# Twelve decoder layers on one core: experts' weights loaded during the routing, two loops of one batch at a time staged side by side, and two steps of a cross-attention moved

## The chip, the core and the metric

The program runs on one core of a Trainium2 chip. The core has a matrix engine (PE, TensorE), a vector engine (DVE, VectorE), an activation engine (ACT, ScalarE), a general engine (POOL, GpSimd) and a queue engine (SP, SyncE) that issues the transfers. Each works through its own instructions in order and waits on semaphores for the others. The metric is the device time of one execution in microseconds (us), lower is better. The time of the kernel before is 4591.87 us, the median of 3 runs (4589.37 to 4594.4).

## What is computed

The reference runs x (16 batches of 128 rows by 256) through twelve sublayers, each `x = x + f(layernorm(x))`. The change touches four of them:

```
# L1_xattn: queries, keys, values from x and ctx rounded to fp8 steps, two attentions (over x, over ctx)
out = [attention(q, k, v), attention(qx, kx, vx)] @ wproj          # 16 + 16 heads of 128
# L1_ffn: one matrix of weights -1, 0, 1, input rounded to 8 bits
y = round(rmsnorm(x) * 127 / peak) @ ternary(W)
# L3_xattn: retention; A sums the scores over the batches, so all batches come before any output
A = max(abs(sum_over_batches(scores * decay)), 1);  out = relu(x @ wg) * groupnorm(A @ V) @ wo
# L3_ffn: 32 experts, 4 for each row, 32 places in each; the places are filled in the order of the rows
xe[expert, place] = x[row];  ye = (silu(xe @ Wg) * (xe @ Wu)) @ Wd;  out = shared(x) + sum(share * ye)
```

## The kernel before

`build_program` calls one function for each sublayer. All of x stays in on-chip memory (`kit.x`, `x_sb` in the profile), and a sublayer updates it in place, batch by batch. A `Phase` holds the tiles and semaphores of a stage; when it is closed, POOL clears the semaphores and all engines meet at a barrier. Within a stage every engine has a loop over the batches of its own (`Fori`), and the order is as written. `staged_by(eng, turn, lead)` calls a body for batches -lead to 15, two in each turn of the loop, so that a body can work on batch b, b+1 and b+2 in one call. `step(...)` makes DVE wait until its instruction has landed.

`L1_ffn` (from L1595) goes through one batch at a time: DVE normalises (L172), scales (L1653), quantises to `q` (L1418 to L1423), PE turns q (L1382), ACT copies it (L1635), PE multiplies (L1625), and DVE adds the result to x (L1657). Then the next batch begins.

`L1_xattn` (from L2492) has a long body for one batch. In its first half PE makes 12 groups of four heads (`make`, L2594) and four groups of values (`make_v`, L2600), DVE scales them to `hat`, PE turns them (`flip`, L2616), and ACT copies them to `hatT` (L2740). In the second half, eight groups m of four heads go through scores (L2624), maxima (L2910), exponentials (L2751, into a tile that the profile names `square`), the turn of P (L2634), its copy (L2757), the product with v (`mix`, L2642), the reciprocals of the sums (L2917), the rounding of the output and the projection. The queries of batch b+1 are turned by PE (`turn_x`, L1382) and copied with a scale by DVE (L2880) inside this half.

`L3_xattn` (from L2298) has two phases. The first loops over the batches and adds up the scores in two banks that stay open; context comes by one DMA per batch into one tile, and SP loads the next when the products of the last are made. The second phase loops again and makes the output; it is already staged by two.

`L3_ffn` (from L2970) has three phases: `L3r` routes (ranks the experts, finds the places, and gathers rows into `fill` banks by one-hot products), `L3e` runs the experts in 8 groups of four, with two slots for a group's weights, and `L3c` brings the results back and adds the shared expert.

Of the kernel before, what the change touches and what calls it, by code (L numbers as in the profile page):

```python
# [1594 lines left out]
def L1_ffn(kit):  # L1595
# [3 lines left out]
    with ExitStack() as ctx:  # L1599
# [6 lines left out]
        peak, scale = ph.sb("peak", [128, 1]), ph.sb("scale", [128, 1])  # L1606
# [9 lines left out]
        @block.tensor  # L1616
        def _(pe):
            w.tensor(kit, pe, bank[0][:, 0:1])
            pe.wait_ge(weights_ready, 1)
            with pe.Fori(0, B) as b:  # L1620
                pe.wait_ge(q_ready.sem, q_ready.after(b))
                turn_bf16(kit, pe, bank[1][:, 0:128].bitcast(BF16), q, C).then_inc(q_turned.sem, 1)
                pe.wait_ge(qT_ready.sem, qT_ready.after(b))
                for k in range(C):
                    last = pe.matmul(bank[2][:, 0:D], qT[:, k, :], w.q[:, k, :], start=(k == 0), stop=(k == C - 1))  # L1625
                last.then_inc(y_made.sem, 1)
# [11 lines left out]
        def _(dve):  # L1638
# [11 lines left out]
            with dve.Fori(0, B) as b:  # L1650
                step.restart()
                step(norm_vector(kit, dve, b, kit.xn[:, :]))
                step(dve.scalar_tensor_tensor(kit.xn[:, :], kit.xn[:, :], rms[:, bass.ds(b, 1)], gamma[:, :], ALU.mult, ALU.mult))  # L1653
                quantize_vector(dve, step, kit.xn[:, :], q[:, :], peak[:, :], scale[:, :], ALU.add, EPS).then_inc(q_ready.sem, 1)
                step(dve.tensor_scalar(peak[:, :], peak[:, :], 1.0 / 127.0, w.unit[:, :], ALU.mult, ALU.mult))
                dve.wait_ge(y_made.sem, y_made.after(b))
                step(dve.scalar_tensor_tensor(kit.x[:, bass.ds(b, 1), :], bank[2][:, 0:D], peak[:, :],  # L1657
                                              kit.x[:, bass.ds(b, 1), :], ALU.mult, ALU.add))
# [639 lines left out]
def L3_xattn(kit):  # L2298
# [4 lines left out]
    with ExitStack() as ctx:  # L2303
# [6 lines left out]
        qT, kT, ctxT = ph.sb("qT", [128, H, 128]), ph.sb("kT", [128, H, 128]), ph.sb("ctxT", [128, C, 128])  # L2310
# [7 lines left out]
        @block.sync  # L2318
        def _(sp):
            sp.dma_start(wh[:, :, :], kit.dram["L3_xattn_Wh"].rearrange("h p n -> p h n")).then_inc(loaded, 16)  # L2320
            sp.dma_start(decay[:, :, :], kit.dram["c_retention"]).then_inc(loaded, 16)
            with sp.Fori(0, B) as b:
                load_batch_T(sp, ctxT, kit.dram, b).then_inc(batch_loaded.sem, 16)
                end_turn(sp, qk_made, b, turns)

        @block.tensor
        def _(pe):
# [4 lines left out]
            with pe.Fori(0, B) as b:  # L2332
                pe.wait_ge(normed.sem, normed.after(b))
                turn_tensor(kit, pe, bank[0], kit.xn).then_inc(turned.sem, 1)
                pe.wait_ge(xT_ready.sem, xT_ready.after(b))
                pe.wait_ge(batch_loaded.sem, batch_loaded.after(b))
                for h in range(H):
                    pe.matmul(bank[1][:, h * 128:(h + 1) * 128], wh[:, h, :], kit.xnT[:, h, :], start=True, stop=True)
                    last = pe.matmul(bank[2][:, h * 128:(h + 1) * 128], wh[:, h, :], ctxT[:, h, :], start=True, stop=True)
                last.then_inc(qk_made.sem, 1)  # L2340
                pe.wait_ge(q_ready.sem, q_ready.after(b))
                pe.wait_ge(k_ready.sem, k_ready.after(b))
                for h in range(H):
                    last = pe.matmul(sums[h], kT[:, h, :], qT[:, h, :], start=False, stop=False)  # L2344
                last.then_inc(used.sem, 1)
# [5 lines left out]
        def _(act):  # L2351
            pre_norm.scalar(act)
            with act.Fori(0, B) as b:
                act.wait_ge(turned.sem, turned.after(b))
                act.copy(kit.xnT[:, :, :], bank[0][:, 0:D]).then_inc(xT_ready.sem, 1)
                act.wait_ge(qk_made.sem, qk_made.after(b))
                act.copy(qT[:, :, :], bank[1][:, 0:D]).then_inc(q_ready.sem, 1)

        @block.vector
        def _(dve):  # L2360
# [3 lines left out]
            with dve.Fori(0, B) as b:  # L2364
                norm_vector(kit, dve, b, kit.xn[:, :]).then_inc(normed.sem, 1)
                dve.wait_ge(qk_made.sem, qk_made.after(b))
                dve.tensor_copy(kT[:, :, :], bank[2][:, 0:D]).then_inc(k_ready.sem, 1)
                dve.wait_ge(used.sem, used.after(b))
# [23 lines left out]
        def _(sp):  # L2392
# [4 lines left out]
            with sp.Fori(0, B) as b:  # L2397
                load_batch_T(sp, ctxT, kit.dram, b).then_inc(batch_loaded2.sem, 16)
                end_turn(sp, v_made, b, turns)

        @second.tensor
        def _(pe):
# [3 lines left out]
            def turn(b, odd, at_b):  # L2406
                ahead, entering = 0 <= at_b + 1 < B, at_b + 2 < B
                if entering:
# [3 lines left out]
                    for h in range(H):  # L2412
                        last = pe.matmul(bank[1][:, h * 128:(h + 1) * 128], ctxT[:, h, :], wh[:, h, :], start=True, stop=True)
# [78 lines left out]
def L1_xattn(kit):  # L2492
# [12 lines left out]
    with ExitStack() as ctx:  # L2505
# [40 lines left out]
        v_bank = (bank[7], bank[0], bank[7], bank[0])  # L2546
# [25 lines left out]
        def _(pe):  # L2572
# [37 lines left out]
            def batch(b, last_batch=False):  # L2610
# [52 lines left out]
                for n in range(4, NG):  # L2663
# [10 lines left out]
                    if n >= 10:  # L2674
                        pe.wait_ge(v_ready.sem, v_ready.after(b, n - 9))
                        make_v(n - 8)
# [4 lines left out]
                flip(NG - 1)  # L2681
# [773 lines left out]
```

## Time and profile before

| | us |
|---|---|
| median of 3 runs | 4591.87 |
| the profiled execution's own time | 4596.84 |
| its span, first to last instruction | 4594.7 |
| PE busy, DVE busy, ACT busy in the span | 3417.8, 2701.4, 1742.3 |
| `L1_xattn`: turned queries copied, first and last batch | 1418.5, 2568.4 |
| `L1_ffn`: first statistics to last update | 2683.2 to 2786.1 |
| `L3_xattn`: first phase, second phase | 3776.1 to 3885.1, 3885.6 to 3976.1 |
| `L3_ffn`: routing, experts, bringing back begins | 3977.8 to 4222.3, 4223.3 to 4348.7, 4349.5 |

The span is what the profiler saw of one execution; the execution's own time has the start and the end around it, 2.1 us here. Starts are counted from the span's beginning. "Busy" of PE is modelled for the end of a matmul, so rows of PE overlap by a little.

### The profile page before, as it was taken

To read this page: it belongs to the slowest core of one execution; us is meant where nothing else is said; L and a number is where in the kernel's file an instruction comes from. 1 tells how busy PE (TensorE), PEld (TensorE's weight loads), DVE (VectorE), ACT (ScalarE), POOL (GpSimd) and SP (SyncE) were. 2 spreads that over 40 slices of the span, in tenths; PEclk is the share of its full clock that TensorE was granted. 3 is DMA by queue.
4 is the path that set the end of the run, shared out by engine and by line. 5 is a ranking of instruction groups with operands and counts; after the bars stand their busy time and mean duration, and the time that the engine had idled before them with its cause. 6 is when DMAs were issued, how large, how long until landed. Compare 5 with 4: busy or idle time off the path is not lost. (4 is left out here: it accounts for less than half of the span.)

```text
span 4594.7 us, 79435 instructions
## 1 busy us (share of the span) xinstructions
PE 3417.8 (74%) x29440; PEld 2478.0 (54%) x29440; DVE 2701.4 (59%) x6762; ACT 1742.3 (38%) x3873; POOL 87.5 (2%) x85
## 2 busy tenths in 40 slices
PE   5588888343776989898988936867767976665798
PEld 4455555211554666665656524656666754433687
DVE  4445555688667767676777666666722761675032
ACT  2233333366224666666666622233322431200011
POOL 0000000000000000000000000000000000000000
PEclk9799999655887999999999967977888995866599
DMA  0000000000300000000000000000000000001400
GB/s 30 30 19 19 20 19 14 32 0 0 126 9 2 1 2 1 2 1 2 1 2 1 1 4 17 4 23 11 9 20 22 0 4 29 24 0 38 132 0 18
DMA packets 85790, 79.54 MB, mean 17 GB/s; under 512 B 12704, under 2 KB 78849, under 8 KB 85121
## 3 DMA queue, kind: packets, MB, share of 16 engines
q1 hardware_dynamic: 85632, 77.21, 5.5%
q8 instruction: 127, 2.08, 0.2%
q14 instruction: 31, 0.25, 0.0%
HBM read 75.09 MB, written 2.10 MB: 17 GB/s over the span
## 5 line engine op out<-in xcount | busy, mean ns | idle before, releaser
L2594 PE MATMUL bank<-L1w_w,L1x_xqT 128*128 128x512 f32 x640 | 305.4, 601 | 1.4 <-DVE L1x_xqT L2880 1.4
L2657 PE MATMUL bank<-L1w_wp,L1x_catT 128*128 128x256 f32 x1024 | 247.4, 385 | 13.2 <-ACT L1x_catT L2768 13.2
L180 PE MATMUL bank<-ident,xn 128*128 128x128 f32 x320 | 77.4, 328 | 219.8 <-DVE xn L172 210.2
L2886 DVE TENSOR_REDUCE L1x_ssq<-L1x_square 128x4 f32<-128x512 f32 x192 | 131.6, 685 | 145.9 <-ACT L1x_square L2730 142.0
L2657 PEld LDWEIGHTS bank<-L1w_wp,L1x_catT 128*128 128x128 f32 x1024 | 188.5, 193 | 43.9 <-ACT L1x_catT L2768 16.1
L760 ACT ACTIVATE L0x_P<-bank 128x512 f32<-128x512 f32 x256 | 132.2, 602 | 190.3 <-PE bank L710 190.3
L2762 ACT ACTIVATE L1x_cat<-bank,L1x_osum 128x128 f32<-128x128 f32 x512 | 146.4, 368 | 152.6 <-DVE L1x_osum L2917 152.6
L776 DVE TENSOR_REDUCE L0x_top<-bank 128x4 f32<-128x512 f32 x256 | 159.0, 684 | 73.4 <-PE bank L688 71.6
L180 PEld LDWEIGHTS bank<-ident,xn 128*128 128x128 f32 x320 | 36.7, 154 | 272.0 <-issue 119.9
L2730 ACT ACTIVATE L1x_square<-bank 128x512 f32<-128x512 f32 x192 | 115.3, 600 | 155.8 <-PE bank L2594 155.8
L2594 PEld LDWEIGHTS bank<-L1w_w,L1x_xqT 128*128 128x128 f32 x640 | 114.0, 192 | 97.1 <-issue 91.4
L2740 ACT ACTIVATE L1x_hatT<-bank,L1x_affine 128x512 f32<-128x512 f32 x192 | 148.6, 774 | 39.3 <-PE bank L2616 37.3
L2616 PEld LDWEIGHTS bank<-ident,L1x_hat 128*128 128x128 f32 x768 | 88.7, 141 | 135.1 <-DVE L1x_hat L2896 96.0
L613 DVE TENSOR_TENSOR x_sb<-x_sb,bank 128x256 f32 (+1 forms) x112 | 47.0, 419 | 193.2 <-PE bank L197 186.6
L172 DVE TENSOR_SCALAR xn<-x_sb,meanvar,rstd 128x256 f32 (+1 forms) x208 | 87.7, 422 | 110.6 <-PE bank L2344 28.3
L2751 ACT ACTIVATE L1x_square<-bank,L1x_top 128x128 f32<-128x128 f32 x512 | 148.5, 397 | 0.0
L2616 PE MATMUL bank<-ident,L1x_hat 128*128 128x128 f32 x768 | 119.4, 278 | 33.9 <-DVE L1x_hat L2896 33.4
L2642 PE MATMUL bank<-L1x_v,L1x_PT 128*128 128x129 f32 x1024 | 140.3, 281 | 0.0
L2924 DVE TENSOR_TENSOR L1x_cat<-L1x_cat,L1x_smooth 128x512 f32<-128x512 f32 x128 | 88.6, 692 | 86.0 <-ACT L1x_cat L2762 86.0
L2896 DVE TENSOR_TENSOR L1x_hat<-bank,L1x_inv 128x512 f32<-128x512 f32 x192 | 132.8, 692 | 9.3
L2624 PE MATMUL bank<-L1x_hatT 128*128 128x128 f32 x1024 | 136.9, 279 | 0.0
L3039 PE MATMUL bank<-L3r_send,L3r_xn 128*128 128x512 f32 x128 | 102.8, 978 | 42.2 <-DVEq L3115 42.2
(642 smaller groups left out, 8173.7 us busy)
## 6 DMA issues: line engine op xcount, KB each, us to landing
L0x_mask<-in_maskrows SPq DMA_DIRECT2D x16, 512.0 KB, 3.6
L3e_wg<-in_L_ffn_Wg SPq DMA_DIRECT2D x8, 704.0 KB, 4.6
L3e_wu<-in_L_ffn_Wu SPq DMA_DIRECT2D x8, 704.0 KB, 6.5
L1w_wp<-in_L_xattn_wproj SPq DMA_DIRECT2D x1, 4096.0 KB, 29.8
L3x_ctxT<-in_ctxT SPq DMA_DIRECT2D x32, 128.0 KB, 2.1
L3e_wd<-in_L_ffn_Wd SPq DMA_DIRECT2D x8, 512.0 KB, 7.8
x_sb<-in_x SPq DMA_DIRECT2D x16, 128.0 KB, 2.2
L0x_ctxT<-in_ctxT SPq DMA_DIRECT2D x16, 128.0 KB, 2.2
```

The costliest lines, as they stand in the source:

```text
L760: act.activation(self.P[:, i % 2, r, :], self.work_bank[r][:, :], ACT.Exp).then_inc(self.p_ready.sem, 1)
L776: dve.tensor_reduce(self.top[:, s, 16 * c + 4 * r:16 * c + 4 * r + 4], self.work_bank[r][:, :].rearrange("p (h k) -> p h k", h=4), X, ALU.max,
L2594: last = pe.matmul(made_bank[n % 4][:, :], inputs(SOURCE[n], k), w[:, k, 4 * n:4 * n + 4, :], start=(k == 0), stop=(k == C - 1))
L2616: last = pe.transpose(flip_bank[n % 2][:, j * 128:(j + 1) * 128], hat[:, n % 2, j * 128:(j + 1) * 128], kit.ident[:, :])
L2624: last = pe.matmul(made_bank[m % 2][:, j * 128:(j + 1) * 128], hatT[:, q, :], hatT[:, k, :], start=True, stop=True)
L2642: last = pe.matmul(mix_bank[j // 2][:, (j % 2) * (d + 1):(j % 2 + 1) * (d + 1)], PT[:, m % 2, j * 128:(j + 1) * 128], v[:, g, :], start=Tr ...
L2657: last = pe.matmul(y_bank[:, 0:D], catT[:, j, :], wp[:, 4 * m + j, :], start=(m == 0 and j == 0), stop=(m == MG - 1 and j == 3))
L2740: act.activation(hatT[:, 4 * n:4 * n + 4, :], flip_bank[n % 2][:, :], ACT.Identity, scale=affine[:, 0, KIND[n]:KIND[n] + 1], bias=affine[: ...
L2751: last = act.activation(P[:, m % 2, j * 128:(j + 1) * 128], made_bank[m % 2][:, j * 128:(j + 1) * 128], ACT.Exp, bias=top[:, 4 * m + j:4 * ...
L2762: last = act.activation(cat[:, j * d:(j + 1) * d], mix_bank[j // 2][:, (j % 2) * (d + 1):(j % 2) * (d + 1) + d], ACT.Copy, scale=osum[:, j ...
L2886: dve.tensor_reduce(ssq[:, 4 * n:4 * n + 4], square[:, n % 2, :].rearrange("p (h e) -> p h e", h=4), X, ALU.add).then_inc(sum_ready.sem, 1)
L2896: dve.tensor_tensor(hat[:, n % 2, :].rearrange("p (h e) -> p h e", h=4), made_bank[n % 4][:, :].rearrange("p (h e) -> p h e", h=4), part.u ...
```

## The change

Five edits in four sublayers. (1) `L1_ffn` is staged by one: DVE prepares batch b+1 before it adds batch b; `peak` and the output bank are doubled. (2) In `L1_xattn` the last value product and the turn of the next batch's queries come after the last flip and ahead of the first turn of P; ACT keeps the last value group after the exponentials of m = 1; DVE copies the turned queries after the first two maxima; banks of the value groups 2 and 3 change places. (3) The first phase of `L3_xattn` is staged by two, with `qT`, `kT` and `ctxT` doubled; a load waits for the load before it and for the products of two batches back. The second phase uses the doubled `ctxT`. (4) In `L3_ffn` the weights have seven slots, in a phase `L3w` of their own around `L3r` and `L3e`; seven groups are loaded by SP during the routing, behind POOL's clearing of `wd1`, the eighth in `L3e`. (5) `L3e` is written out for the 8 groups, with two banks each for hidden and output; PE makes hidden(g+1) before it projects group g, and reads `xeT` directly.

```diff
@@ L1_ffn, tensor @@
-            with pe.Fori(0, B) as b:
+            with pe.Fori(0, B // 2) as t:
+                for i in range(2):
+                    b = t * 2 + i
...
-                    last = pe.matmul(bank[2][:, 0:D], qT[:, k, :], w.q[:, k, :], ...)
+                        last = pe.matmul(bank[2 + i][:, 0:D], qT[:, k, :], w.q[:, k, :], ...)
@@ L1_ffn, vector @@
+            def turn(b, odd, at_b):
+                here, ahead = at_b >= 0, at_b + 1 < B
                 step.restart()
+                if ahead:
+                    step(norm_vector(kit, dve, b + 1, kit.xn[:, :]))
+                    step(dve.scalar_tensor_tensor(kit.xn[:, :], kit.xn[:, :], rms[:, bass.ds(b + 1, 1)], gamma[:, :], ...))
+                    if here:
+                        dve.wait_ge(q_turned.sem, q_turned.after(b))
+                    part = peak[:, 1 - odd:2 - odd]
+                    quantize_vector(...).then_inc(q_ready.sem, 1)
+                    step(dve.tensor_scalar(part, part, 1.0 / 127.0, w.unit[:, :], ALU.mult, ALU.mult))
+                if here:
+                    dve.wait_ge(y_made.sem, y_made.after(b))
+                    step(dve.scalar_tensor_tensor(kit.x[:, bass.ds(b, 1), :], bank[2 + odd][:, 0:D], ...))
+            staged_by(dve, turn, 1)
@@ L3_xattn, sync (the second phase alike, with v_made) @@
-            with sp.Fori(0, B) as b:
-                load_batch_T(sp, ctxT, kit.dram, b).then_inc(batch_loaded.sem, 16)
-                end_turn(sp, qk_made, b, turns)
+            load(0, 0, batch_loaded)
+            sp.wait_ge(batch_loaded.sem, batch_loaded.after(0))
+            load(1, 1, batch_loaded)
+            with sp.Fori(0, (B - 2) // 2) as t:
+                for i in range(2):
+                    b = t * 2 + i
+                    sp.wait_ge(batch_loaded.sem, batch_loaded.after(b + 1))
+                    sp.sem_inc(turns, 1)
+                    sp.wait_ge(qk_made.sem, qk_made.after(b))
+                    sp.sem_inc(turns, 1)
+                    load(b + 2, i, batch_loaded)
@@ L3_xattn, scalar and vector @@
+                if ahead:
+                    act.wait_ge(qk_made.sem, qk_made.after(b + 1))
+                    act.copy(qT[:, 1 - odd, :, :], bank[1][:, 0:D]).then_inc(q_ready.sem, 1)
+                if entering:
+                    act.wait_ge(turned.sem, turned.after(b + 2))
+                    act.copy(kit.xnT[:, :, :], bank[0][:, 0:D]).then_inc(xT_ready.sem, 1)
...
+                    norm_vector(kit, dve, b + 2, kit.xn[:, :]).then_inc(normed.sem, 1)
+                if ahead:
+                    dve.wait_ge(qk_made.sem, qk_made.after(b + 1))
+                    dve.tensor_copy(kT[:, 1 - odd, :, :], bank[2][:, 0:D]).then_inc(k_ready.sem, 1)
@@ L1_xattn @@
-        v_bank = (bank[7], bank[0], bank[7], bank[0])
+        v_bank = (bank[7], bank[0], bank[0], bank[7])
...
                 flip(NG - 1)
+                pe.wait_ge(v_ready.sem, v_ready.after(b, 1))
+                make_v(3)
+                if not last_batch:
+                    pe.wait_ge(v_ready.sem, v_ready.after(b, 3))
+                    turn_x(b + 1)
                 turn_p(0)
... scalar
                 exponentials(1)
+                keep_v(3)
                 turn_p(0)
... vector
                 maxima(1)
+                if not last_batch:
+                    turn_x(b + 1)
                 for m in range(MG):
...
-                    if m == 0 and not last_batch:
-                        turn_x(b + 1)
@@ L3_ffn @@
+        SLOTS = GROUPS - 1
+        wg, wu = (wx.sb(n, [128, SLOTS, PER, C, F]) for n in ("wg", "wu"))
...
+                sp.wait_ge(wd1_cleared, 1)
+                for g in range(SLOTS):
+                    load_group(sp, g)
+            @block.gpsimd
+            def _(pool):
+                pool.memset(wd1[:, :, :, :], 0.0).then_inc(wd1_cleared, 1)
... experts, tensor
+                pe.wait_ge(cleared, 1)
+                hidden(0)
+                for g in range(GROUPS):
+                    if g + 1 < GROUPS:
+                        hidden(g + 1)
+                    pe.wait_ge(gu_ready, g + 1)
+                    if g >= 2:
+                        pe.wait_ge(out_ready, g - 1)
+                    ...    # the 8 projections of group g, into out_bank[g % 2]
+                    last.then_inc(out_made, 1)
+        experts.close()
```

On PE, in the second half of a batch of `L1_xattn`: `hatT` times `hatT` are the scores, `square` is P, `yb` the queries of the next batch, and the product of `w` and `ctxT` is the last value group. Before, from the last value product to the first product with v:

```order
L2600 MATMUL bank<-L1w_w,L1x_ctxT 128x512 x2
L2612 REGISTER_ALU
L2616 MATMUL bank<-ident,L1x_hat 128x128 x4
L2624 MATMUL bank<-L1x_hatT 128x128 x8
...
L2616 MATMUL bank<-ident,L1x_hat 128x128 x4
L2628 ISA
L2634 MATMUL bank<-ident,L1x_square 128x128 x4
...
L2642 MATMUL bank<-L1x_v,L1x_PT 128x129 x4
L2586 REGISTER_ALU
L1382 MATMUL bank<-identb,L1x_yb 128x128 x8
```

After, the same stretch (line numbers have moved by 58):

```order
L2674 MATMUL bank<-ident,L1x_hat 128x128 x4
L2682 MATMUL bank<-L1x_hatT 128x128 x8
...
L2674 MATMUL bank<-ident,L1x_hat 128x128 x4
L2740 REGISTER_ALU
L2658 MATMUL bank<-L1w_w,L1x_ctxT 128x512 x2
L2743 REGISTER_ALU
L2644 REGISTER_ALU
L1382 MATMUL bank<-identb,L1x_yb 128x128 x8
L2686 ISA
L2692 MATMUL bank<-ident,L1x_square 128x128 x4
```

The value product has moved behind the scores and the last flips, and the turn of `yb` from behind the first product with v to a place ahead of the first turn of P.

On PE, in the loop of the first phase of `L3_xattn`: `xn` turned, four products with `wh`, and the sums `kT` times `qT`. Before, one batch in a turn of the loop, all of the same batch:

```order
L2332 ISA
L180 MATMUL bank<-ident,xn 128x128 x2
L2336 ISA
L2338 MATMUL bank<-xnT,L3x_wh 128x128
L2339 MATMUL bank<-L3x_ctxT,L3x_wh 128x128
...
L2344 MATMUL bank<-L3x_qT,L3x_kT 128x128 x2
L2332 REGISTER_ALU
L2332 COMPARE_AND_BRANCH
```

After, the second half of a turn of the loop, which holds two such pieces:

```order
L2360 ISA
L2365 MATMUL bank<-xnT,L3x_wh 128x128
L2366 MATMUL bank<-L3x_ctxT,L3x_wh 128x128
...
L2369 REGISTER_ALU
L180 MATMUL bank<-ident,xn 128x128 x2
L2375 MATMUL bank<-L3x_qT,L3x_kT 128x128 x2
L605 REGISTER_ALU
L605 COMPARE_AND_BRANCH
```

The turn of `xn` stands behind the four products now, and belongs to the batch after theirs, the sums to the batch ahead of theirs.

On DVE, in the loop of `L1_ffn`, before, from the quantised `q` to the loop's end:

```order
L1423 TENSOR_SCALAR L1f_q<-xn 128x256
L1655 TENSOR_SCALAR L1f_peak<-L1f_peak,L1f_w_unit 128x1
L1656 REGISTER_ALU
L1657 SCALAR_TENSOR_TENSOR x_sb<-bank,L1f_peak,x_sb 128x256
L1650 REGISTER_ALU
L1650 COMPARE_AND_BRANCH
```

After, from the update of x in the first half of a turn of the loop:

```order
L1666 SCALAR_TENSOR_TENSOR x_sb<-bank,L1f_peak,x_sb 128x256
L41 ISA
L172 ISA x2
L172 TENSOR_SCALAR xn<-x_sb,meanvar,rstd 128x256
L1658 REGISTER_ALU
L1658 SCALAR_TENSOR_TENSOR xn<-xn,L1f_rms,L1f_gamma 128x256
...
L1423 TENSOR_SCALAR L1f_q<-xn 128x256
L1663 TENSOR_SCALAR L1f_peak<-L1f_peak,L1f_w_unit 128x1
L1666 SCALAR_TENSOR_TENSOR x_sb<-bank,L1f_peak,x_sb 128x256
L605 REGISTER_ALU
L605 COMPARE_AND_BRANCH
```

The engine's instructions are the same; the update now is that of the batch before the one just quantised, and the loop closes once for two batches.

## Rows read from the trace of the kernel before

**Rows 1.** Busy us by stage: start:end, us, engines, PEclk, DMA share, GB/s.

```profile
2697.00:2786.00 89.00, 16.06 (x64) 4.21 (x64) 48.35 (x160) 5.96 (x16) 0.00 (x0) 0.50 0.00 0
3785.00:3884.00 99.00, 64.96 (x232) 49.70 (x232) 13.63 (x33) 11.92 (x32) 0.00 (x0) 0.50 0.07 20
4236.00:4246.00 10.00, 9.88 (x64) 9.55 (x64) 0.00 (x0) 0.08 (x1) 0.00 (x0) 0.50 0.63 173
```

**Rows 2.** Tile L1f_q by line; timeline (start, us, idle before) of L1_ffn and L3m.

```profile
L1423 DVE TENSOR_SCALAR L1f_q<-xn x16: 294/294/294, 2699.2 to 2783.8; 128x256 bf16<-128x256 f32 x16
...
2701.07 0.48 DVE L1657 SCALAR_TENSOR_TENSOR x_sb<-bank,L1f_peak,x_sb 128x256 f32 x1 [1.44 <-PE bank L1625]
...
3904.86 0.41 DVE L172 TENSOR_SCALAR xn<-x_sb,meanvar,rstd 128x256 f32 x1 [0.58 <-DVE L3m_y L2480]
...
3910.08 0.41 DVE L172 TENSOR_SCALAR xn<-x_sb,meanvar,rstd 128x256 f32 x1 [0.93 <-DVE L3m_y L2480]
```

**Rows 3.** Timeline of one batch of L1_xattn, PE, ACT and DVE.

```profile
2319.65 1.88 PE L2600 MATMUL bank<-L1w_w,L1x_ctxT 128*128 128x512 f32 x4
...
2326.64 0.66 PE L2634 MATMUL bank<-ident,L1x_square 128*128 128x128 f32 x4 [1.25 <-ACT L1x_square L2751]
...
2328.11 0.65 ACT L2757 COPY L1x_PT<-bank 128x512 f32<-128x512 f32 x1
...
2329.82 0.61 PE L1382 MATMUL bank<-identb,L1x_yb 128*128 128x128 bf16 x8
2330.02 0.38 DVE L2917 RECIPROCAL L1x_osum<-bank 128x2 f32<-128x2 f32 x2 [4.87 <-PE bank L2642]
...
2334.37 1.22 DVE L2880 TENSOR_TENSOR L1x_xqT<-bank,L1x_in_scale 128x1024 f32<-128x1024 bf16 x1
2335.51 0.36 DVE L2917 RECIPROCAL L1x_osum<-bank 128x2 f32<-128x2 f32 x2
...
2339.85 0.38 DVE L2917 RECIPROCAL L1x_osum<-bank 128x2 f32<-128x2 f32 x2
```

**Rows 4.** Tile L3x_qT by line; timeline of L3_xattn, both phases, PE and SP.

```profile
L2357 ACT COPY L3x_qT<-bank x16: 372/372/373, 3789.2 to 3881.0; 128x256 f32<-128x256 f32 x16
...
3794.27 0.64 PE L2338 MATMUL bank<-xnT,L3x_wh 128*128 128x128 f32 x2
3794.70 0.63 PE L2339 MATMUL bank<-L3x_ctxT,L3x_wh 128*128 128x128 f32 x2
...
3887.72 7.01 SPq L2096 DMA_DIRECT2D L3x_ctxT<-in_ctxT  x2
...
3892.78 1.06 PE L2413 MATMUL bank<-L3x_wh,L3x_ctxT 128*128 128x128 f32 x4
3897.11 0.71 PE L2413 MATMUL bank<-L3x_wh,L3x_ctxT 128*128 128x128 f32 x4 [0.64 <-DMA L3x_ctxT<-in_ctxT]
```

**Rows 5.** Timeline of the experts: start, first group, end.

```profile
4223.31 0.27 DVE L3188 MEMSET L3e_gu<- 128x256 f32 x1 [0.99 <-PEq L89]
...
4235.87 5.04 PE L3166 MATMUL bank<-L3e_xg,L3e_wg 128*128 128x32 f32 x32 [16.95 <-DMA L3e_wd<-in_L_ffn_Wd]
...
4246.91 1.94 PE L3172 MATMUL bank<-L3e_wd,L3e_gu 128*32 128x256 f32 x16 [1.03 <-DVE L3e_gu L3196]
...
4348.31 0.37 ACT L3184 COPY L3f_ye<-bank 128x256 f32 x1 [2.65 <-PE bank L3172]
```

**Rows 6.** Line L2821 by engine; timeline of the routing's start, DVE.

```profile
L2821 POOL TENSOR_TENSOR L1w_w<-L1w_w,L1x_center x1: 10454/10454/10454, 1394.4 to 1394.4; 128x6144 f32<-128x6144 f32 x1
L2821 DVE TENSOR_TENSOR L1w_w<-L1w_w,L1x_center x1: 16856/16856/16856, 1394.4 to 1394.4; 128x6144 f32<-128x6144 f32 x1
...
3977.84 5.33 DVE L156 BATCH_NORM_STATS2 stat<-x_sb  x16 [1.74 <-PEq L89]
...
3983.65 0.18 DVE L163 TENSOR_SCALAR meanvar<-meanvar 128x16 f32<-128x16 f32 x1
```

**Rows 7.** Line L1152 in two stretches: us, DVE busy, PEclk, DMA share, GB/s.

```profile
1165.00:1200.00 35.00, 4.97 (x8) 0.85 1.02 377
1200.00:1260.00 60.00, 14.91 (x24) 1.00 0.01 2
```

More of the change, by code:

```diff
@@ L2331, in _, with turn @@
                 pe.matmul(sums[h], zero[:, :], zero[:, :], start=True, stop=False)
[L2332 to L2345, printed above, removed]
+            def turn(b, odd, at_b):
+                here, ahead, entering = at_b >= 0, 0 <= at_b + 1 < B, at_b + 2 < B
+                if ahead:
+                    pe.wait_ge(xT_ready.sem, xT_ready.after(b + 1))
+                    pe.wait_ge(batch_loaded.sem, batch_loaded.after(b + 1))
+                    if here:
+                        pe.wait_ge(q_ready.sem, q_ready.after(b))
+                        pe.wait_ge(k_ready.sem, k_ready.after(b))
+                    for h in range(H):
+                        pe.matmul(bank[1][:, h * 128:(h + 1) * 128], wh[:, h, :], kit.xnT[:, h, :], start=True, stop=True)
+                        last = pe.matmul(bank[2][:, h * 128:(h + 1) * 128], wh[:, h, :], ctxT[:, 1 - odd, h, :], start=True, stop=True)
+                    last.then_inc(qk_made.sem, 1)
+                if entering:
+                    pe.wait_ge(normed.sem, normed.after(b + 2))
+                    turn_tensor(kit, pe, bank[0], kit.xn).then_inc(turned.sem, 1)
+                if here:
+                    pe.wait_ge(q_ready.sem, q_ready.after(b))
+                    pe.wait_ge(k_ready.sem, k_ready.after(b))
+                    for h in range(H):
+                        last = pe.matmul(sums[h], kT[:, odd, h, :], qT[:, odd, h, :], start=False, stop=False)
+                    last.then_inc(used.sem, 1)
@@ L2352, in _, with turn @@
             pre_norm.scalar(act)
[L2353 to L2357, printed above, removed]
+            def turn(b, odd, at_b):
+                ahead, entering = 0 <= at_b + 1 < B, at_b + 2 < B
+                if ahead:
+                    act.wait_ge(qk_made.sem, qk_made.after(b + 1))
+                    act.copy(qT[:, 1 - odd, :, :], bank[1][:, 0:D]).then_inc(q_ready.sem, 1)
+                if entering:
+                    act.wait_ge(turned.sem, turned.after(b + 2))
+                    act.copy(kit.xnT[:, :, :], bank[0][:, 0:D]).then_inc(xT_ready.sem, 1)
+            staged_by(act, turn, 2)
         @block.vector
@@ L3186, in _ @@
+                silu(0)
+                for g in range(GROUPS):
+                    if g + 1 < GROUPS:
+                        silu(g + 1)
+                    act.wait_ge(out_made, g + 1)
+                    act.copy(ye[:, g, :], out_bank[g % 2][:, 0:D]).then_inc(out_ready, 1)
             @block.vector
             def _(dve):
-                dve.memset(gu[:, :, :], 0.0).then_inc(cleared, 1)
-                dve.memset(wd1[:, :, :, :], 0.0).then_inc(cleared, 1)
-                dve.wait_ge(cleared, 2)
```

173 lines of the change are left out of this document (90 added, 83 removed).

## The prediction

> **What bounds the kernel now.** I read the engines' busy time by stage first. The program is twelve layers one after the other with a barrier between their phases, so a gain in one stage is a gain in the whole, and each stage has to be asked what ends last in it. The change touches four stages of layer 1 and layer 3. [Rows 1] show two that no engine fills: in layer 1's feed-forward PE is busy 16.06 of 89 us and DVE 48.35; in the retention sums PE is busy 64.96 of 99. In the experts PE is 9.88 of 10 us busy inside a group, yet at half clock. Then I read the timeline of one batch in each stage, for the waits that repeat.
>
> **Feed-forward of layer 1.** One batch takes (2783.8 - 2699.2) / 15 = 5.64 us. The residual update waits 1.44 us for PE, while q is turned, copied and multiplied [rows 2]. Afterwards DVE normalises and quantises batch b+1 before it asks for y of b, so that wait is gone but for the 0.05 between neighbours: 1.39 per batch. Two batches stand in one turn of the loop. Another paired loop shows 0.58 and 0.93 us in turn ahead of its first instruction [rows 2], so a loop's turn costs 0.35, and half of it is saved: 0.17. I charge 0.08 for the added wait on q_turned and register work. 1.48 x 15 = 22.2 us less. Bounds: 18 if the new waits cost 0.3 per batch, 26 if the whole 0.35 goes. What is late next is DVE itself, at about 4.16 us per batch; PE's 1.4 us lie beside it.
>
> **Cross-attention of layer 1, 15 of 16 batches.** The scaled copy of the turned queries (L2880, 1.22 us on DVE) stands between the first and the second head group: these are 2335.51 - 2330.02 = 5.49 apart, the next two 4.34 [rows 3]. So its removal gives 1.15, since DVE idles 4.87 us before 2330.02 and can take it there. What pays is the path to the first product. PE now makes the last value product (L2600, 1.88 us) and turns the queries (0.61) before it turns P, where it idled 1.25 [rows 3]. By their starts these are about 1.7 + 0.45 = 2.15 of issue, so P is turned some 0.3 to 0.9 late; the score product behind it was waiting for ACT anyway, and takes most of that up. On ACT the copy of v (L2745) now stands just ahead of the copy of P (L2757 at 2328.11, 0.65 for the same 128x512 from PSUM), and nothing covers it: the first product starts about 0.6 later. Net 0.55 x 15 = 8.2 us less. Bounds: 17 if PE's and ACT's additions are wholly covered, a loss of 5 if both add (0.9 + 0.6 - 1.15 = 0.35 x 15). In its old place the value product cost nothing: the flip behind it waited for DVE's hat. SP's context load now waits for a later v_made, but is needed half a batch after.
>
> **Retention sums of layer 3.** A batch takes (3881.0 - 3789.2) / 15 = 6.12 us, a strict ring of norm, turn, copy, eight products, copy, sums [rows 4]. Afterwards the products of b+1, the turn of b+2 and the sums of b stand in a row on PE, and all copies run beside. Two chains are then left. PE: 14 instructions, which start 0.21 us apart at 1.2 GHz (3794.27 to 3794.70 for two), 2.98 us. SP: load b+2 is issued only when load b+1 has landed, so the loads stand one behind the other. From the end of the value product (3892.78 + 1.06 = 3893.84) to the issue it released (3887.72 + 7.01 - 0.37 = 3894.36) pass 0.52, and from there to PE's start on that data (3897.11) 2.75: 3.27 per load at most, some of it PE's own reaction [rows 4]. I take 3.2 us per batch: 2.92 x 15 = 43.8 less. Bounds: 2.6 us (a landing of 2.1 and 0.5 to issue, PE at full clock), 52.8 less; and 4.2 (one more handing-on from DVE to PE like the 1.03 of [rows 5], beside some slack), 28.8 less. If PE's clock rises here it gains little, since the loads hold it. In the second half of the stage the doubled context takes away one wait of 0.64, 0.6 less.
>
> **Experts.** Before, the stage runs from 4223.31 to 4348.68, 125.4 us: 12.6 until the first weights are there, then groups in which PE makes hidden products for 10.0 us (4235.87 to 4246.91 - 1.03), waits 1.03 for gu, and projects down [rows 5]. The 16 projections end 1.94 after the first starts, 0.63 of it the last one's own, so four rounds of 0.44: 1.74 of issue. Afterwards seven of eight groups' weights (14.8 MB) are loaded during the routing, and PE goes from hidden(g+1) to down(g) without a wait: 0.5 for the cleared gu, 8 x 11.7 = 93.6 (the last hidden product's own end lies under the first projection), 0.6 for the last result and its copy, 94.7. That is 30.7 less. One more phase is closed, a clear and a barrier, 0.5. So 30.2; bounds 28 (0.3 per group at each change) and 31. Group 7's load is issued after the second projection, over 40 us before its use.
>
> Does the clock rise when PE's pauses go? In [rows 1] a stretch of 10 us that is 9.88 busy stays at 0.50, which is 1.2 GHz. The hidden products are 32 columns wide with weight loads between, and their pace is the load's. The Trainium skill (TensorE: Matmul & The Clock Gate, § Why this matters for your kernels) advises to keep TensorE busy without a break to get the full clock; by that rule the stage would gain again. The row speaks against it here; I keep it as a rival.
>
> **Routing.** New is GpSimd's clearing of wd1, 7168 elements wide, at the start of the stage, beside DVE's statistics. Where both worked on w, DVE's instruction of the same shape as GpSimd's took 16.86 us against 10.45 [rows 6]: DVE stood while GpSimd had the memory. If the clearing costs per element what that row shows, it takes 12.2 us from 3977.8: 12.2 more if it holds DVE from the first statistics on, 6.3 if it holds it from 3983.65 on, and nothing if it holds nothing or ends before. It only writes, where that one reads twice and writes, so it should be nearer to half as long and in the way of less, and I take 1.5 us more. The Trainium skill (SBUF — State Buffer, § Who interferes with whom) says that the second to come waits for the whole instruction, though a GpSimd instruction that only writes holds just DVE's two-port forms, as the tensor_scalar at 3983.65 would be; by that 6.3 would be the most, and a clearing of 6 us would cost nothing. The transfers themselves I cost at nothing: DVE's reduction took 4.97 / 8 = 0.62 us at a DMA share of 1.02 and 14.91 / 24 = 0.62 at 0.01 [rows 7]. At the 173 GB/s of [rows 1] they are done within 90 of the stage's 244 us.
>
> **Sum**, against the profiled execution's own time of 4596.84 (span 4594.7): -22.2 - 8.2 - 43.8 - 0.6 - 30.2 + 1.5 = -103.5, so 4493.3. The median of the runs shown is 5.0 lower, 4591.87; the same step down gives 4488.
>
> **Rivals.**
> - The experts' clock rises to 2.4 GHz. For it: no pause is left. Against it: [rows 1]. Weight loads and products at half their time make 93.6 some 50, 43 less: 4445.
> - The retention loop does not overlap as written; one wait per batch stays and it runs at 4.2: 15 x 1.0 more, 4503. For it: serial loads and four engines handing on within 3 us. Against it: each handed-on step is ready one turn earlier.
> - Layer 1's moves do not do what they say: the first product is later by 1.5 against the 1.15 won. 13 more, 4501. For it: ACT's copy sits uncovered in the chain. Against it: PE's 1.25 idle.
> - Slower than before: the weight traffic slows the routing. Its place is the 244 us from 3977.8; its price must pass 103.5 us to decide, so every batch there would have to stretch by over 40%, also after the transfers have ended; at 45% it costs 110, 4598. For it: 14.8 MB where nothing was moved. Against it: [rows 7], and no instruction of the routing waits for SP.
>
> **How the numbers follow.** Forecast 64%, fast clock 7%, slow retention loop 14%, layer 1 without gain 12%, slower 3%. The likeliest is 4488, its own range 4470 to 4502. Taking in the second and third rival and the bounds of the loop (2.6 to 4.2 us, +-15), of GpSimd's clearing (to +11) and of layer 1 gives 4464 to 4512; outside lie the first and the last and the tails. A measurement here tells a difference of 0.2%, 9 us. Faster by more: 0.96; within: 0.01; slower: 0.03.
>
> **What would show it.** In the changed profile: quantisations of layer 1's feed-forward 4.1 to 4.2 us apart with no wait for PE at the residual; in the cross-attention the first two reciprocals 4.3 apart and the first product some 0.6 later after the last flip; retention copies 3.2 us apart, with PE released by the context's DMA; experts' groups 11.7 apart at granted clock 0.50; DVE's reductions in the routing as long as before. I am wrong if the retention copies are over 4 or the groups under 10 us apart, if the routing has grown by more than 6 us, or if a stage the change doesn't touch moves by more than 3.

## The result, and the profile after

The changed kernel takes 4485.85 us (median of 4 runs, 4482.73 to 4489.16), against 4593.14 for the kernel before on the same chip (4589.37 to 4596.66): a ratio of 0.9767, 95% interval 0.975 to 0.9784. Its profiled execution took 4488.55, with a span of 4486.5, where 4493.3 was forecast (4488 for the median). The sum came out; its terms did not all. Stages are counted here from one stage's first DMA issue to the next one's (the experts from DVE's clearing of their first tile, 4223.3 and 4149.6), in the two profiled executions:

| stage | before | after | difference | forecast |
|---|---|---|---|---|
| all ahead of layer 1's cross-attention | 1358.7 | 1356.7 | -2.0 | 0 |
| cross-attention of layer 1 | 1324.2 | 1325.4 | +1.2 | -8.2 |
| feed-forward of layer 1 | 104.0 | 80.1 | -23.9 | -22.2 |
| layer 2, self-attention of layer 3 (not touched) | 988.8 | 995.2 | +6.4 | 0 |
| retention, first phase | 109.9 | 53.7 | -56.2 | -43.8 |
| retention, second phase | 91.9 | 91.3 | -0.6 | -0.6 |
| routing | 245.8 | 247.2 | +1.4 | +1.5 |
| experts | 126.2 | 90.7 | -35.5 | -30.2 |
| shared expert and store (not touched) | 245.2 | 246.2 | +1.0 | 0 |
| span | 4594.7 | 4486.5 | -108.2 | -103.5 |

Busy time by stretch in the changed kernel (start:end, us, busy us of PE, PEld, DVE, ACT, POOL, then PEclk, DMA share, GB/s), which answers to [rows 1]:

```profile
2697.00:2761.00 64.00, 16.05 (x64) 4.22 (x64) 47.00 (x157) 5.96 (x16) 0.00 (x0) 0.50 0.00 0
3771.00:3810.00 39.00, 28.34 (x218) 25.24 (x216) 13.13 (x33) 10.03 (x31) 0.00 (x0) 1.00 0.16 48
4150.00:4239.00 89.00, 88.67 (x640) 76.94 (x640) 3.92 (x17) 6.89 (x25) 0.00 (x0) 0.54 0.09 25
```

The feed-forward is now filled by DVE (47.00 of 64). The retention sums run at the full clock from 3771.0 on, where they had 0.50 throughout before. The experts' PE is busy without a gap, at 0.54.

**Cross-attention.** The timeline of one batch (start, us, idle before), PE, then ACT, then DVE; the rows of before are [rows 3]:

```profile
1767.74 0.66 PE L2674 MATMUL bank<-ident,L1x_hat 128*128 128x128 f32 x4 [2.05 <-DVE L1x_hat L2958]
...
1773.05 0.61 PE L2692 MATMUL bank<-ident,L1x_square 128*128 128x128 f32 x4
1774.71 1.16 PE L2682 MATMUL bank<-L1x_hatT 128*128 128x128 f32 x8 [1.05 <-ACT L1x_v L2806]
...
1776.14 1.06 PE L2700 MATMUL bank<-L1x_v,L1x_PT 128*128 128x129 f32 x8
...
1773.99 0.66 ACT L2806 ACTIVATE L1x_v<-bank 128x512 f32<-128x512 f32 x1
1774.47 0.66 ACT L2818 COPY L1x_PT<-bank 128x512 f32<-128x512 f32 x1
...
1769.14 0.69 DVE L2958 TENSOR_TENSOR L1x_hat<-bank,L1x_inv 128x512 f32<-128x512 f32 x1
...
1777.24 0.37 DVE L2979 RECIPROCAL L1x_osum<-bank 128x2 f32<-128x2 f32 x2 [2.76 <-PE bank L2700]
...
1781.59 0.37 DVE L2979 RECIPROCAL L1x_osum<-bank 128x2 f32<-128x2 f32 x2
```

The first two reciprocals are 4.35 apart, as forecast (5.49 before). But from the batch's last hat (1769.14) to the first reciprocal (1777.24) pass 8.10 us; before it was 6.76 (2323.26 to 2330.02 in the batch of [rows 3], whose last hat is the first row below). PE turned P, and then stood 1.05 us ahead of the *score* product until ACT had copied v. A batch is 1.34 longer here and 1.14 shorter there: 78.22 us instead of 78.02, 3.0 over 15, and the first batch adds its own 1.3. The stage is only 1.2 longer, since PE's clock fell four times in it before, at 7.9 us in all, and three times now, at 4.9. The falls of before lie behind the turn of the rounded output, which waited 1.53 us for DVE's copy of the queries (1.2 to 2.8 us each); here are that turn and the stretch with one fall, in the kernel before:

```profile
2323.26 0.69 DVE L2896 TENSOR_TENSOR L1x_hat<-bank,L1x_inv 128x512 f32<-128x512 f32 x1
...
1941.69 0.38 PE L1382 MATMUL bank<-identb,L1x_catb 128*128 128x128 bf16 x4 [1.53 <-DVE L1x_xqT L2880]
...
1943.50:1947.50 4.00, 3.41 (x16) 3.33 (x17) 2.53 (x9) 1.66 (x6) 0.00 (x0) 0.57 0.00 0
```

The falls of the changed kernel lie elsewhere, behind the 2.05 in the first row of the cross-attention above; of these more below.

**Retention sums.** The tile's row, and the timeline of one period on PE and SP, against [rows 4]:

```profile
L2391 ACT COPY L3x_qT<-bank x16: 372/373/373, 3770.9 to 3807.5; 128x256 f32<-128x256 f32 x16
...
3778.07 0.49 PE L2365 MATMUL bank<-xnT,L3x_wh 128*128 128x128 f32 x2 [0.28 <-DMA L3x_ctxT<-in_ctxT]
3778.34 2.75 SPq L2107 DMA_DIRECT2D L3x_ctxT<-in_ctxT  x2
...
3780.45 0.49 PE L2365 MATMUL bank<-xnT,L3x_wh 128*128 128x128 f32 x2 [0.55 <-DMA L3x_ctxT<-in_ctxT]
```

The copies are (3807.5 - 3770.9) / 15 = 2.44 us apart, and what PE waits for is the context's DMA. SP issues a load, and the next one 2.75 - 0.37 = 2.38 later; over the phase these distances are 2.35 to 2.54, and once 3.63. The first four copies are 2.05 to 2.17 apart, ahead of the point where the loads set the pace.

**Feed-forward, routing, experts.** The quantisations' row and a residual without a wait [rows 2]; the clearing beside the statistics and the first group's load [rows 6]; one group of the experts on PE [rows 5]:

```profile
L1423 DVE TENSOR_SCALAR L1f_q<-xn x16: 293/294/295, 2697.9 to 2759.0; 128x256 bf16<-128x256 f32 x16
...
2714.45 0.48 DVE L1666 SCALAR_TENSOR_TENSOR x_sb<-bank,L1f_peak,x_sb 128x256 f32 x1
...
3902.37 6.07 POOL L3098 MEMSET L3w_wd<- 128x7168 f32 x1 [416.96 <-POOLq L89]
3902.71 5.33 DVE L156 BATCH_NORM_STATS2 stat<-x_sb  x16 [1.75 <-PEq L89]
3908.47 0.38 SPq L3063 DMA_DIRECT2D L3w_wg<-in_L_ffn_Wg  x1
...
4213.51 5.04 PE L3237 MATMUL bank<-L3f_xeT,L3w_wg 128*128 128x32 f32 x32
...
4223.46 1.94 PE L3251 MATMUL bank<-L3w_wd,L3e_gu 128*32 128x256 f32 x16
4225.33 1.06 PE L3237 MATMUL bank<-L3f_xeT,L3w_wg 128*128 128x32 f32 x4
```

4.07 us per batch in the feed-forward; a clearing of 6.07 us that leaves the statistics at 5.33, as they were; a group of 4225.33 - 4213.51 = 11.82. But not all groups are alike: from 4184.0 and from 4204.5 on, PE is granted the full clock for 3.4 us each, as this stretch shows, and the hidden products in which these fall take 7.1 us instead of 9.95. Those two groups take 9.0 us, under the 10 that the prediction named as a sign of being wrong.

```profile
4184.00:4187.00 3.00, 3.00 (x36) 2.92 (x36) 0.00 (x0) 0.24 (x1) 0.00 (x0) 1.00 0.00 0
```

### The profile page after: what moved, and what is told of

Read it like the earlier page. It is cut to its first block and busy times, and to the rows that moved or that the text cites. A ratio compares the mean times of both kernels' runs of the same rounds, so it can differ in the third digit from the quotient of the medians.

```text
span 4486.5 us, 79321 instructions
## 1 busy us (share of the span) xinstructions
PE 3375.0 (75%) x29440; PEld 2453.1 (55%) x29440; DVE 2699.9 (60%) x6753; ACT 1735.3 (39%) x3870; POOL 94.1 (2%) x86
## 3 DMA queue, kind: packets, MB, share of 16 engines
q8 instruction: 131, 2.15, 0.2%
## 5 line engine op out<-in xcount | busy, mean ns | idle before, releaser
L2682 PEld LDWEIGHTS bank<-L1x_hatT 128*128 128x128 f32 x1024 | 127.5, 198 | 21.1 <-ACT L1x_v L2806 21.1
```

Source lines behind the costliest of these rows:

```text
L2682: last = pe.matmul(made_bank[m % 2][:, j * 128:(j + 1) * 128], hatT[:, q, :], hatT[:, k, :], start=True, stop=True)
```

## The experiments

All start from the changed kernel except the last; times are own times, of single executions where no interval is given. "Batch" is the distance of the first reciprocals of two batches of the cross-attention.

**The wait for v moved behind the score product** (e1).

```diff
                 turn_p(0)
-                pe.wait_ge(v_ready.sem, v_ready.after(b))
                 for m in range(MG):
...
                         turn_p(m + 1)
+                    if m == 0:
+                        pe.wait_ge(v_ready.sem, v_ready.after(b))
                     mix(m)
```

> The changed kernel, with PE's wait for the last value copy moved from ahead of score product 2 to just ahead of the first P-times-V product of a batch. Theory A (that wait is what ate the gain: PE stands 1.05 us at the score product until ACT has copied v, and only then makes the score product, turns P and multiplies, 1.43 us one behind the other; moved, the score product lies beside ACT's copy, and the first product starts when ACT's first copy of P is there, 0.85 to 1.0 us earlier): from the last hat to the first reciprocal 7.1 to 7.25 us instead of 8.10, batches 77.3 apart instead of 78.2, 13 to 15 us less in all, about 4472. Theory B (ACT alone is the chain: exponentials, copy of v, two copies of P): less than 0.3 us per batch, 4481 or more.

4475.04 us (4471.39 to 4483.39, 4 runs), ratio to before 0.9742 (0.9724 to 0.9761). PE and DVE in one batch:

```profile
1772.32 1.06 PE L2682 MATMUL bank<-L1x_hatT 128*128 128x128 f32 x8
1774.10 1.13 PE L2700 MATMUL bank<-L1x_v,L1x_PT 128*128 128x129 f32 x8 [0.29 <-ACT L1x_PT L2819]
...
1767.96 0.69 DVE L2959 TENSOR_TENSOR L1x_hat<-bank,L1x_inv 128x512 f32<-128x512 f32 x1
...
1775.27 0.38 DVE L2980 RECIPROCAL L1x_osum<-bank 128x2 f32<-128x2 f32 x2 [1.96 <-PE bank L2700]
```

Theory A holds for the chain: the wait of 1.05 is gone, what is left is 0.29 for ACT's copy of P, and hat to reciprocal takes 7.31 instead of 8.10. A batch is 77.42 where nothing disturbs it. It doesn't hold for the stage, which is 1.4 us shorter instead of 13 to 15: ten of the 16 batches take 1.63 more, because the clock falls in them. One stretch around such a fall:

```profile
1844.00:1848.00 4.00, 4.00 (x22) 4.00 (x23) 2.63 (x7) 1.51 (x3) 0.00 (x0) 0.57 0.00 0
```

It falls just after the pause of PE ahead of the flips that wait for hat, which is the first row shown of the cross-attention above (2.05 us), and the 16 score products take 3.50 us instead of 1.95. That pause was 0.33 before the change, since the value product lay in it. In the changed kernel the clock falls so in 3 batches, and in each of the four other runs that have its cross-attention unchanged (e4 to e7) also in 3. The rest of the 10.8 us by which this kernel is faster came in stages that it does not touch.

**The value product back in its old place, the queries still early** (e2).

```diff
                         make_v(2)
+                    if n == 11:
+                        make_v(3)
...
                 flip(NG - 1)
-                pe.wait_ge(v_ready.sem, v_ready.after(b, 1))
-                make_v(3)
```

and on ACT `keep_v(3)` goes back in the same way.

> The changed kernel, with the last value product and its copy back in their old place after the last made group, the turned queries still early. Theory A (the value product in the chain costs 1.34 us per batch, the early queries give 1.15 and cost nothing, since PE's 0.45 us of turning fit into its 1.25 idle): last hat to first reciprocal 6.76 as before the change, first two reciprocals 4.35 apart, batches 76.9 apart, 20 us less than the changed kernel, about 4466. Rival (turning the queries ahead of P delays the chain too): 0.3 to 0.45 per batch of it lost, 77.3, 4472.

4453.16 us (4449.06 to 4458.77, 4 runs), ratio 0.9689 (0.9672 to 0.9705). PE around the flips, DVE's last hat and first two reciprocals, and the stage:

```profile
1761.14 1.88 PE L2658 MATMUL bank<-L1w_w,L1x_ctxT 128*128 128x512 f32 x4
1763.35 0.66 PE L2674 MATMUL bank<-ident,L1x_hat 128*128 128x128 f32 x4 [0.33 <-DVE L1x_hat L2957]
...
1768.13 0.66 PE L2692 MATMUL bank<-ident,L1x_square 128*128 128x128 f32 x4 [0.80 <-ACT L1x_square L2812]
...
1764.75 0.69 DVE L2957 TENSOR_TENSOR L1x_hat<-bank,L1x_inv 128x512 f32<-128x512 f32 x1
...
1771.50 0.37 DVE L2978 RECIPROCAL L1x_osum<-bank 128x2 f32<-128x2 f32 x2 [2.91 <-PE bank L2700]
1775.84 0.38 DVE L2978 RECIPROCAL L1x_osum<-bank 128x2 f32<-128x2 f32 x2
...
1424.00:2655.00 1231.00, 1114.43 (x6003) 778.51 (x6001) 875.55 (x2086) 800.21 (x1981) 0.00 (x0) 1.00 0.01 2
```

Theory A holds: 6.75 from hat to reciprocal, 4.34 between the first two, 76.83 per batch. PE turns the queries within its pause, of which 0.80 is left. And the gain is larger than expected, 27.3 us of the stage, since the clock never falls in it: 15 x 1.39 = 20.9, the first batch's own 1.35, and three falls of 1.6. This version beats both kernels.

**Only the value product moved** (e3): PE's and DVE's `turn_x` back behind the first product and its quantisation.

```diff
                     mix(m)
+                    if m == 0 and not last_batch:
+                        turn_x(b + 1)
```

> The changed kernel, with the turned queries (PE's and DVE's part) back in their old place after the first product, the value product still moved. Theory A (the value product alone costs the 1.34 us): last hat to first reciprocal still 8.1, first two reciprocals 5.49 apart, batches 79.35 apart, 17 us more than the changed kernel, about 4503. Rival (PE's turning of the queries ahead of P is a part of the 1.34): last hat to first reciprocal 7.65, batches 78.9, 4496.

4505.99 us, one execution. Last hat and the first two reciprocals of one batch on DVE:

```profile
1772.33 0.69 DVE L2957 TENSOR_TENSOR L1x_hat<-bank,L1x_inv 128x512 f32<-128x512 f32 x1
1780.42 0.37 DVE L2978 RECIPROCAL L1x_osum<-bank 128x2 f32<-128x2 f32 x2 [6.21 <-PE bank L2700]
...
1785.91 0.36 DVE L2978 RECIPROCAL L1x_osum<-bank 128x2 f32<-128x2 f32 x2
```

8.09 and 5.49, 79.33 in an undisturbed batch: the value product alone costs the 1.34, and the early queries add nothing to it. The rival is out. Ten intervals lost 1.3 to 2.8 us to the clock besides. Its falls are of both sorts: eight lie where those of the changed kernel do, four where those of the kernel before do.

**Context loads that don't wait for each other** (e4), in both phases of the retention; PE waits on a semaphore per buffer.

```diff
-                    sp.wait_ge(batch_loaded.sem, batch_loaded.after(b + 1))
-                    sp.sem_inc(turns, 1)
                     sp.wait_ge(qk_made.sem, qk_made.after(b))
                     sp.sem_inc(turns, 1)
-                    load(b + 2, i, batch_loaded)
+                    load(b + 2, i)
```

> The changed kernel, with the context loads of layer 3's two phases on a semaphore per buffer, so that load b+2 is issued when the products of b are done and no longer waits for the landing of load b+1. Theory A (the loads, one behind the other, set the 2.44 us between the retention copies; PE's own chain of 14 instructions and the copy of xnT end 1.75 to 1.85 after a batch's first product at 2.4 GHz): copies 1.85 to 2.0 apart once the clock is up, first phase 6 to 8.5 us shorter, second phase within 1, about 4478. Theory B (the handing on between PE, ACT and DVE sets the pace as well): copies 2.3 or more apart, 4484.

4476.5 us (4472.84 to 4488.14, 4 runs), ratio 0.975 (0.9734 to 0.9766). ACT's copies of the queries, and what PE waited for later in the phase (us in total, times, longest):

```profile
3772.51 0.37 ACT L2388 COPY L3x_qT<-bank 128x256 f32<-128x256 f32 x1 [2.17 <-PE bank L2363]
3775.72 0.37 ACT L2388 COPY L3x_qT<-bank 128x256 f32<-128x256 f32 x1 [2.42 <-PE bank L2363]
3778.84 0.37 ACT L2388 COPY L3x_qT<-bank 128x256 f32<-128x256 f32 x1 [2.32 <-PE bank L2363]
3781.20 0.37 ACT L2388 COPY L3x_qT<-bank 128x256 f32<-128x256 f32 x1 [1.56 <-PE bank L2363]
...
PE bank L2362 <- ACT xnT L2391: 3.3, 11, 0.4
```

Between the theories. The loads did set the 2.44: without their chain the copies are 2.10 apart (2.05 and 2.15 in turn), and PE waits for ACT's copy of xnT instead. But that ring is longer than theory A had it, and the phase is 3.0 us shorter, not 6 to 8.5. Even that is rough: with the loads chained as in the changed kernel the phase took 52.1 to 55.3 us in six kernels, with the loads apart 50.7 here and 49.7 in the run that has both edits. Until the clock rose, 20.6 us into the phase, the copies were 3.21 and 3.12 apart: that is the pace forecast for the changed kernel, at the clock at which it was forecast.

**One context buffer's worth of order** (e5): load b+1 only after the products of b.

```diff
-                    sp.wait_ge(qk_made.sem, qk_made.after(b))
+                    sp.wait_ge(qk_made.sem, qk_made.after(b + 1))
```

(and load 1 waits for the products of batch 0.)

> The changed kernel, with load b+1 of the retention sums issued only after the products of b, as if there were one context buffer; the engines' overlap stays. Load and products then stand one behind the other: 2.44 for issue and landing, and the eight products, 0.98 at 2.4 GHz or 1.95 at 1.2 GHz. Theory A (PE's longer pauses keep the clock at 1.2 GHz, as before the change): copies 4.4 apart, 29 us more than the changed kernel, 4515. Theory B (the clock rises all the same): 3.4 apart, 15 us more, 4500.

4505.82 us, one execution; the phase takes 72.9 us. Two copies, and the stretch in which they lie:

```profile
3787.58 0.37 ACT L2391 COPY L3x_qT<-bank 128x256 f32<-128x256 f32 x1 [2.79 <-PE bank L2366]
3791.08 0.37 ACT L2391 COPY L3x_qT<-bank 128x256 f32<-128x256 f32 x1 [2.85 <-PE bank L2366]
...
3786.00:3829.00 43.00, 22.77 (x174) 20.34 (x174) 10.08 (x25) 7.48 (x23) 0.00 (x0) 1.00 0.11 34
```

Theory B: the clock rises all the same, and then the copies are 3.5 apart (4.3 to 4.65 ahead of that). So of the 56.2 us of this phase, the overlap of the engines and the clock that came with it gave 37.0, and the second buffer 19.2, each to some 2 us, since the phase moves by that much with its code unchanged.

**Prefetch alone** (e6): the experts' groups one after the other on PE.

```diff
-                hidden(0)
                 for g in range(GROUPS):
-                    if g + 1 < GROUPS:
-                        hidden(g + 1)
+                    hidden(g)
                     pe.wait_ge(gu_ready, g + 1)
```

> The changed kernel, with the experts' groups one after the other on PE (hidden products of a group, wait for gu, projections), and the weights still loaded during the routing. Theory A (the waits for gu go by the order on PE, about 1.0 us per group, and the two short stretches of 2.4 GHz come only where PE has no pause): groups 12.8 apart at a granted clock of 0.50, stage 14 us longer than in the changed kernel, about 4500. Rival (the stretches of 2.4 GHz come with pauses too, each some 2.8 us less): about 4494.

4488.33 us, one execution. PE over one group:

```profile
4159.76 1.94 PE L3249 MATMUL bank<-L3w_wd,L3e_gu 128*32 128x256 f32 x16 [1.03 <-DVE L3e_gu L3278]
...
4172.67 1.94 PE L3249 MATMUL bank<-L3w_wd,L3e_gu 128*32 128x256 f32 x16 [1.03 <-DVE L3e_gu L3278]
...
4146.00:4240.00 94.00, 85.11 (x576) 72.59 (x576) 3.82 (x16) 5.37 (x24) 0.00 (x0) 0.50 0.08 24
```

12.91 per group, the stage 105.5 us, 14.8 more than in the changed kernel: theory A, and the clock stays at 0.50. So the prefetch gave 20.7 of the 35.5 us, the order on PE 14.8, of which 5.7 are the two short rises. The own time is that of the changed kernel's profiled execution, because the stages ahead of the experts took 14.4 us less here without being touched; how far they move is told with the last run.

**No look-ahead in the feed-forward** (e7): DVE's order of before, in the loop of two batches per turn.

```diff
-            staged_by(dve, turn, 1)
+            staged_by(dve, turn, 0)
```

with `turn` making the norm, the quantisation, the wait for y and the residual of one batch b.

> The changed kernel, with DVE's order in layer 1's feed-forward as before the change (norm, quantisation, wait for y, residual of one batch), in the loop of two batches per turn and with two y banks. Theory A (the wait for y of 1.44 us gave nearly all, the paired loop 0.17): quantisations 5.46 apart instead of 4.07, stage 20 to 21 us longer, about 4506. Rival (half of the gain came from the loop's turns): 4.9 apart, 12 us longer, 4498.

4501.04 us, one execution. The quantisations:

```profile
L1423 DVE TENSOR_SCALAR L1f_q<-xn x16: 293/294/295, 2693.2 to 2774.3; 128x256 bf16<-128x256 f32 x16
```

5.41 apart, the stage 20.6 us longer, Theory A. The look-ahead gave 1.34 per batch and the paired loop 0.23, against the 1.39 less 0.08 and the 0.17 of the forecast.

**Value product back and loads apart together** (best1).

> The changed kernel with the value product back in its old place (turned queries still early) and the context loads on a semaphore per buffer: the sum of the two edits. By the first alone 4453 was measured; with the loads apart 6 to 8 us less, about 4446. If the rival on the loads holds, 4452.

4455.63 us (4452.38 to 4457.2, 4 runs), ratio 0.9707 (0.9691 to 0.9723). The cross-attention keeps its 76.88 per batch and the retention copies are 2.1 apart, but the 4446 expected was not reached, and beyond the first edit alone nothing can be told (intervals 0.9672 to 0.9705 and 0.9691 to 0.9723 overlap). The 3 us of the loads are less than these times tell apart.

**The kernel before once more** (before_again).

> The kernel before once more, unchanged, for how far a stage moves from execution to execution. If the 2 to 3 us by which the stages 2786.9 to 2983.1 and 2983.1 to 3344.6 grew in the changed kernel come from it, they are again 196.2 and 361.5 long here, within 0.5; if they are the clock's phase, either can be 2 to 3 us longer.

4595.24 us. Layer 2's self-attention is again 196.2 us long and its cross-attention 361.6. In the nine other profiles these two are 195.9 to 199.0 and 361.0 to 364.4, with the same code. Ahead of the feed-forward this execution is 5.2 us shorter than the first one of the same kernel. So stages move without being touched: those of 196 to 361 us in layers 2 and 3 by 3 to 4 us, layer 0's cross-attention (some 640 us) by 6.6, and several together by 5 to 14. What the longer ones have more of is time at the low clock. Layer 3's self-attention, in the two executions of the kernel before:

```profile
3519.40:3775.70 256.30, 218.94 (x2544) 164.98 (x2544) 189.91 (x579) 104.14 (x193) 0.00 (x0) 0.95 0.03 10
3514.30:3774.30 260.00, 222.94 (x2544) 167.95 (x2544) 189.75 (x579) 104.24 (x193) 0.00 (x0) 0.93 0.03 10
```

The same instructions take 3.7 us more with 37.0 us at 0.50 instead of 26.4. Over all eleven profiles this stage takes 255.9 to 257.2 us with 26 to 28 us at 0.50, and 259.9 to 260.2 with 34 to 37; layer 2's self-attention takes 195.9 to 196.4 with 20 to 22, and 198.1 to 199.0 with 27 to 32. So of the 6.4 us that these stages took more in the changed kernel, 2.7 each in layer 2's two attentions, the clock is the likely cause; why it stays low for longer in one execution than in the next is open.

## Why the prediction came out, point by point

**Cross-attention: the step failed.** The forecast let the first product be 0.6 later for ACT's copy, and said of PE that "the score product behind it was waiting for ACT anyway, and takes most of that up". Two things were overlooked. The wait for all of v stands on PE ahead of that score product, not ahead of the product that needs v; as long as v was ready early it cost nothing. With the copy of v late, ACT's copy and PE's own score and turn no longer lie side by side: 1.34 instead of 0.6, which e1 takes back in part and e2 in whole. And taking the value product from its old place was costed at nothing, because the flip behind it waited for DVE anyway. That wait then became PE's pause of 2.05 us, and behind it the clock fell in 3 batches here and in 10 of e1. In all seven kernels with the value product moved the clock falls there, in none of the four with it in its old place. The other move acted on the clock as well, which the prediction had not counted either: the falls of the kernel before, behind the pause of 1.53 us that DVE's copy of the queries made, come in the three profiles with the queries in their old place (the kernel before twice, and e3) and in none of the eight with them early. So the clock gave 7.9 us and took 4.9; without that the stage would have grown by 4 us. That the falls come of the pauses is an inference: no run changed a pause alone, and the same 2.05 us is followed by 3, 8 or 10 falls. The rival "layer 1's moves do not do what they say" was right in kind and in size: 1.34 against 1.14, with 1.5 against 1.15 written down.

**Retention: mechanism right, mis-sized term.** Forecast 3.2 per batch, measured 2.44, below the lower bound of 2.6. At 1.2 GHz copies are that far apart (3.21 and 3.12 in e4), but in e4 no load waits for the load before it, and with the chain e1 and e7 have 3.13 there: that pace was not the loads'. Wrong was "If PE's clock rises here it gains little, since the loads hold it": it rested on 3.27 us per load, of which 2.75 was read from the issue to PE's start on the data. That load was a slow one: it landed 2.7 us after its issue, where the median of that phase's next 13 is 2.1, so most of what was taken for PE's reaction was its landing. From issue to issue a load takes 2.35 to 2.54. The clock rose 13.6 us into the phase and took PE's 2.98 away; the loads held PE at 2.44 instead of 3.27. 12.4 us more gain.

**Experts: right, with a part of a rival.** 11.82 per group against 11.7, the prefetch and the order on PE as worked out. The clock stayed at 0.50 but for two stretches of 3.4 us, which gave 5.7. They came at the same places, 34.4 and 54.9 us into the stage, in all seven other runs with this order on PE, and not at all in e6, where PE pauses. By the Trainium skill (TensorE: Matmul & The Clock Gate, § Why this matters for your kernels), keeping TensorE busy should have given the full clock. The row says otherwise: 88.67 us busy of 89 at a granted 0.54, and the rival's 43 us were 5.7.

**Feed-forward: right.** 4.07 per batch against 4.16; e7 splits it as forecast.

**Routing: the number right, the reason wrong.** The clearing took 6.07 us and cost nothing: the statistics beside it took 5.33 as before, and the two small instructions beside its end 0.19 each as before. The Trainium skill (SBUF — State Buffer, § Who interferes with whom) says that beside a GpSimd instruction that only writes, DVE is held in its two-port forms alone. The trace agrees as far as it goes: the first tensor_scalar starts at 3908.51, 0.07 us behind the clearing's end, so no run shows what becomes of one beside it. The bound of 12.2 from [rows 6] was no measure for an instruction that only writes. The +1.4 lies within what this stage does by itself: 244.9 to 247.2 us in the nine kernels with the clearing, 245.8 twice without it. DVE's reductions over 128x1024 took 1.22 us each, before and after, so nothing came of the slower side.

**Why the sum held.** Retention gave 12.4 more and the experts 5.3 more, the feed-forward 1.7; the cross-attention gave 9.4 less, and untouched stages took 5.4. The forecast of 4488 was not more exact than that: errors of 9 to 12 us cancelled, and that the total came within 5 us is luck.

## What to carry to other kernels

A wait in front of a group of instructions is free only as long as its signal is early; before a producer is moved later, look where its consumers' wait stands, and move it to the instruction that needs the data. Work that fills a pause of PE isn't worthless because it ends no wait: ask what PE's pause will be without it, and what the clock does then. And where a ring is unrolled, work its length out at both clocks, with a load's time taken from issue to issue.

## What was not expected of the hardware

- Behind a pause of 2.05 us PE's granted clock fell to 0.50 for a stretch in 10 of 16 batches when a batch took 77.4 us, in 3 when it took 78.2, and in none of e2's, where it was 0.33 (76.8 us). The kernel before had 0.33 there too, and its clock fell four times at another place, behind a pause of 1.53 us.
- In the retention sums the clock rose to 1.00 within 13.4 to 27.7 us of the phase's start in every kernel with the engines overlapped, even in e5, where PE waits for a load in each batch, and never in the ring of before [rows 1].
- The experts' products kept PE at 0.54 over 89 us without a gap.
- A GpSimd clearing of 128x7168 took 6.07 us and did not slow DVE's statistics beside it.
- The same 2544 products of an untouched stage took 256.3 or 260.0 us in two executions of one kernel, with 26.4 and 37.0 us at a granted 0.50.
